# Scores in four PSUM banks, three attention groups a batch, and the context sum carried as one row by DMA

## The chip, the cores and the metric

The kernel runs on one core of one Trainium2 chip. The metric is the device time of one execution in microseconds (us). The engines named below are PE (TensorE: matrix products), DVE (VectorE), ACT (ScalarE), POOL (GpSimd) and SP (SyncE, which here only issues DMAs). ACT issues DMAs too, from a queue of its own. PSUM has eight banks of 128 partitions x 512 fp32 columns; PE writes there, and DVE and ACT read it.

## The reference, cut to what matters

There are 16 batches of 256 tokens and 512 features. Each batch goes through a gated linear attention with 8 heads, a residual and a layer norm; then it is multiplied by a decayed running sum of the squared context, with a residual and a layer norm again. A feed-forward stage with 8 experts follows; it takes over half of the time and the change does not touch it. The running sum is this part:

```
kv = jnp.swapaxes(k * v, 0, 1)          # k = v = ctx_1024: the square of the context
def step(r, kv_t):
    r = DECAY * r + kv_t                # DECAY = 0.9, over the 256 tokens of a batch
    return (r, r)
_, rs = jax.lax.scan(step, r0, kv)
return q * jnp.swapaxes(rs, 0, 1)
```

The attention is `M = M * f_t + g_t * scale * k_t v_t`, `y_t = (q_t M) * o_t`. The kernel writes it as scores k q, weighted with decays, times v.

## The kernel before

**Steps.** The attention stage is a pipeline over batches. Step b (`body(b)` on each engine) projects batch b (q, k, v, gates) and attends batch b-1, projects it out, and ends batch b-2 (layer norms, product with the sum). Steps 2 to 13 are a loop of two steps an iteration, the others are written out. Each engine runs its own list in order; semaphores join the lists.

**PE in one step.** 24 shares of projection (`project_share(b, g)`, g = 0 to 23) in the order k, k, v, q, q, v: a q or k share is six products of 256 columns, a v share three of 512. All are made of fp32 parts: high by high, high by low, low by high (`exact_product`). Between shares stand the pieces of attention: `scores(b-1, c)` for a pair of heads c = 0 to 3, into the two banks `turn`, and `weighted_values(b-1, c)` into `y_ps` and `s_ps`. Before the change PE leaves the projection for attention five times a step: scores 0; scores 1 and values 0; scores 2 and values 1; scores 3 and values 2; values 3. Then come the gate products of batch b+1, the six products of `cross_memory(b-1)` and `project_out(b-1)` (24 products of 512 columns).

**The context sum.** ACT squares the context (`square_ctx`, in place in `c_sb`) and makes its high part `ctx_hi`; POOL makes the low part `ctx_lo` (`context_low`). `cross_memory` sums over tokens by products with a triangle of ones, `sums[:, 0]`; the first 128 tokens also go into the second 128 by two products with a square of ones, `sums[:, 1]`. ACT scales the sums back into `c_sb` (`grow_memory`), and PE may overwrite the bank only after that (`mem_grown`).

**DVE** weights the scores of a head with its decays into `probs` (`weigh`), scans the decays of the next batch (`scans`), multiplies q and k by the rope tables (`rope_parts`), and makes the low parts of y (`y_low`) and of the sums' residuals. **POOL** makes the rope tables with the output gate (`o_tables`) and rotates q and k: `rotate(b, 0)` and `(b, 1)` are k, `(b, 2)` and `(b, 3)` are q.

**SP** issues its DMAs in a fixed order. In step b: `store_rms(b+1)` (256 single fp32 numbers from SBUF to DRAM, `rms_dram`), the loads of x and xT of batch b+2 and of the context of batch b, a store of batch b-2 (`x_dram`), `spread_rms(b+1)` (`rms_rows`, which waits until the stores of `store_rms` have landed), then `move(b, 0)`, `move(b, 2)`, `move(b, 1)`, `move(b, 3)` (four DMAs each, `qkT<-rot`, where `move(b, r)` waits for `rotate(b, r)`), and `following(b+1)`: `store_o`, `spread_f`, `load_g`, `spread_o` (`o_dram`, `f_all`, `g_raw`, `rot<-o_dram`).

Of the kernel before, what the change touches and what calls it, by code (L numbers as in the profile page):

```python
# [20 lines left out]
F32 = mybir.dt.float32  # L21
# [77 lines left out]
def layer_program(nc, scope, x, xT, ctx_in, norm_w, wT, wgT, bg, woutT, bout, gamma, beta, w1, b1, w2, b2,  # L99
# [91 lines left out]
    shift = sb("shift", [P, NT])  # L191

# [9 lines left out]
    s_ps = bank("s_ps")  # L202
    y_ps = bank("y_ps")
    gate_ps = bank("gate_ps")
# [27 lines left out]
    ctx_hi_done, ctx_lo_done, mem_grown = sem("ctx_hi_done"), sem("ctx_lo_done"), sem("mem_grown")  # L232
    u_done, stats2_done, x2_done, x2_stored = sem("u_done"), sem("stats2_done"), sem("x2_done"), sem("x2_stored")
# [7 lines left out]
    def score_banks(b):  # L241

        return turn

    def value_bank(b, c):

        return (y_ps, s_ps)[c % 2]
# [8 lines left out]

    def memory(b):

        return qk_ps[:, 0:D], qk_ps[:, D:2 * D]
# [109 lines left out]
    with nc.Block() as block:  # L369
# [238 lines left out]
        def _(act):  # L608
# [35 lines left out]
            def y_high(b, c):  # L644
                act.wait_ge(y_mm, b.after(KC, c + 1))
                if b.n >= 1 and c == 0:
                    act.wait_ge(out_mm, (b - 1).after(NT, NT))
                act.activation(yT_hi[:, c, :], value_bank(b, c)[:, 0:L], ACT.Copy).then_inc(y_hi_done, 1)
# [20 lines left out]
            def square_ctx(b):  # L669
# [10 lines left out]
                act.activation(ctx_hi, c_sb[b.odd][:], ACT.Copy).then_inc(ctx_hi_done, 1)  # L680

            def grow_memory(b):

                for j in range(NT):
                    act.wait_ge(mem_mm, b.after(NT, j + 1))
                    if j == 0:
                        act.wait_ge(ctx_lo_done, b.after(1, 1))
                    act.activation(c_sb[b.odd][:, j, :], memory(b)[j], ACT.Identity, bias=one[:],  # L688
                                   scale=grow[:, j:j + 1]).then_inc(mem_grown, 1)
# [9 lines left out]
            def body(b):  # L699
# [37 lines left out]
                if b.n == 1:  # L737
                    grow_memory(b - 1)
# [7 lines left out]
                if (b - 1).within(B) and b.n != 1:  # L746
                    grow_memory(b - 1)
# [76 lines left out]
        def _(pool):  # L824
# [53 lines left out]
            def context_low(b):  # L878
# [3 lines left out]
                pool.tensor_tensor(ctx_lo, c_sb[b.odd][:], ctx_hi.bitcast(F32), ALU.subtract).then_inc(ctx_lo_done, 1)  # L882
# [18 lines left out]
            def rotate(b, r):  # L901
                pool.wait_ge(rope_done, b.after(NB, r + 1))
                if b.n >= 1 and r in (0, 2):
                    pool.wait_ge(s_mm, (b - 1).after(NH, NH // 2 * (r // 2 + 1)))
# [12 lines left out]
            def body(b):  # L917
# [27 lines left out]
                if b.within(B) and b.n >= 1:  # L945
                    rotate(b, 0)
                    rotate(b, 1)
                if b.n == 1:
# [83 lines left out]
        def _(dve):  # L1032
# [49 lines left out]
            def scan(b, n):  # L1082

                dve.wait_ge(f_cleared, b.after(1, 1))
                if b.n >= 1:
                    dve.wait_ge(probs_done, (b - 1).after(NH, n + 1))
# [30 lines left out]
            def weigh(b, n):  # L1117
                dve.wait_ge(s_mm, b.after(NH, n + 1))
                dve.wait_ge(decay_done, b.after(NH, n + 1))
                if n >= 4:  # L1120
                    dve.wait_ge(y_mm, b.after(KC, (n - 4) // 2 + 1))
                elif b.n >= 1:
                    dve.wait_ge(y_mm, (b - 1).after(KC, (n + 4) // 2 + 1))
                dve.tensor_tensor(probs[:, n % 4, :], score_banks(b)[n % 2][:, 0:DW], decays[:, n, :], ALU.mult).then_inc(probs_done, 1)

            def y_low(b, c):
                dve.wait_ge(y_hi_done, b.after(KC, c + 1))
                dve.tensor_tensor(yT_lo[:, c, :], value_bank(b, c)[:, 0:L], yT_hi[:, c, :].bitcast(F32),
                                  ALU.subtract).then_inc(y_lo_done, 1)
# [31 lines left out]

            def weigh_pair(b, c):
                weigh(b, 2 * c)
                weigh(b, 2 * c + 1)
# [38 lines left out]
            def second(b):  # L1203
# [6 lines left out]
                y_low(b - 1, 0)  # L1210
# [5 lines left out]
                y_low(b - 1, 1)  # L1216
# [4 lines left out]
                y_low(b - 1, 2)  # L1221
                rope_parts(b, 2)
                y_low(b - 1, 3)
# [8 lines left out]
            def middle(b, last):  # L1232
                weigh_pair(b - 1, 0)
                add_memory(b - 2)
                norm_stats(b - 2, 1)
                weigh_pair(b - 1, 1)
                rope_parts(b, 0)
                y_low(b - 1, 0)
# [3 lines left out]
                weigh_pair(b - 1, 2)  # L1242
                token_gates(b)
                gate_v(b, 0)
                if last:
                    token_stats()
                    token_means()
                y_low(b - 1, 1)
# [3 lines left out]
                weigh_pair(b - 1, 3)  # L1252
                rope_parts(b, 2)
                y_low(b - 1, 2)
                rope_parts(b, 3)
                scans(b, 4 if last else 6)
                y_low(b - 1, 3)
# [17 lines left out]
            def behind(b):  # L1275
# [5 lines left out]
                y_low(b, 0)  # L1281
                weigh_pair(b, 2)
                add_memory(b - 1)
                y_low(b, 1)
                weigh_pair(b, 3)
                norm_stats(b - 1, 1)
                y_low(b, 2)
                split_hidden(Step(0), 0)
                y_low(b, 3)
# [107 lines left out]
        def _(pe):  # L1397
# [47 lines left out]
            def project_share(b, g):  # L1445
# [14 lines left out]
                elif part == 0 and n == 1 and b.n >= 2:  # L1460
                    pe.wait_ge(mem_grown, (b - 2).after(NT, j + 1))
# [23 lines left out]
            def scores(b, c):  # L1485
# [5 lines left out]
                if c == 0 and b.n >= 1:  # L1491
                    pe.wait_ge(probs_done, (b - 1).after(NH, NH))
                if c >= 1:
                    pe.wait_ge(probs_done, b.after(NH, 2 * c))
                halves = (slice(0, DH), slice(DH, 2 * DH))
                for rows, bank in zip(halves, score_banks(b)):
                    pe.matmul(bank[:, 0:P], kT[rows, c, P:L], qT[rows, c, P:L], start=True, stop=True)
                for rows, bank in zip(halves, score_banks(b)):
# [229 lines left out]
```

## Time and profile before

| | |
|---|---|
| time, median of 3 runs | 1248.84 us (1248.21 to 1250.78) |
| span of the profiled execution | 1250.1 us |
| PE busy | 1230.2 us (98%) |
| DVE, POOL, ACT busy | 780.7, 740.3, 460.8 us |
| steps 2 to 14 of the attention stage | from 67.92 to 496.24 us in the trace |
| two neighbouring steps of the loop begin at | 333.98 and 366.37 us |

The profiled execution's own time is its span; what lies around it is not in the trace. It stands 1.3 us (0.1%) over the median. A busy PE is a PE with a product in flight: products are pipelined, so a wait shorter than some 0.2 us does not show as idle time.

### The profile page before, as it was taken

The page shows a single profiled execution, that of the slowest core. Times are in us where ns is not written, and L with a number is a line of the kernel's source. Part 1 is how long each engine was busy: PE and PEld are TensorE (multiplying, and loading weights), DVE is VectorE, ACT ScalarE, POOL GpSimd, SP SyncE. Part 2 cuts the span into 40 slices and gives each one's busy share as a digit, 9 for nine tenths or more (in the row PEclk, how much of TensorE's full clock was granted, in tenths as well). Part 3 has the DMA queues.
Part 4 walks back from the last instruction along what each step waited for, and adds up shares of the span by engine and source line. Part 5 has one row for each costly group of instructions (what it writes and reads, how often), then busy time and mean ns, then how long its engine had stood idle before and what let it go on. Part 6 is the DMA issues. An engine that isn't in the chain of part 4 may idle for free.

```text
span 1250.1 us, 19325 instructions
## 1 busy us (share of the span) xinstructions
PE 1230.2 (98%) x6682; PEld 1011.4 (81%) x6682; DVE 780.7 (62%) x1297; ACT 460.8 (37%) x629; POOL 740.3 (59%) x519
## 2 busy tenths in 40 slices
PE   8989999999999999999999999999999999999998
PEld 7777888888888888778888888888888888888886
DVE  5887888888888888973544534543734535435424
ACT  5223333333233332353434434433534344343330
POOL 4876566666666666648538357274294385483651
PEclk9999999999999999999999999999999999999999
DMA  8778777777877776636307325235164073163310
GB/s 278 157 152 163 163 160 153 161 163 159 161 155 159 153 141 112 189 128 248 114 10 267 101 84 211 85 138 175 66 208 170 0 277 101 34 246 99 111 59 34
DMA packets 178107, 179.52 MB, mean 144 GB/s; under 512 B 44732, under 2 KB 121484, under 8 KB 178060
## 3 DMA queue, kind: packets, MB, share of 16 engines
q1 hardware_dynamic: 177548, 178.64, 53.3%
q8 instruction: 29, 0.48, 0.1%
q10 hardware_dynamic: 512, 0.26, 0.1%
q14 instruction: 18, 0.15, 0.0%
HBM read 137.55 MB, written 17.18 MB: 124 GB/s over the span
## 4 chain that ended last, share of the span: by engine, by line
PE 57%; DVE 2%; POOL 1%; issue 1%; DMA 0%; ACT 0%; POOLq 0%; DVEq 0%; ACTq 0%
PE qk_ps L89 5%; PE qk_ps L88 5%; PE qk_ps L87 5%; PE v_ps L87 5%; PE v_ps L89 5%; PE v_ps L88 5%; PE gate_ps L87 5%; PE gate_ps L89 5%; PE gate_ps L88 5%; PE s_ps L87 3%; PE s_ps L89 3%; PE s_ps L88 3%; PE y_ps L87 2%; PE y_ps L89 2%; PE y_ps L88 2%
## 5 line engine op out<-in xcount | busy, mean ns | idle before, releaser
L1006 POOL TENSOR_TENSOR w_lo<-w_raw,w_hi 128x2048 fp32r<-128x2048 f32 x31 | 143.2, 4620 | 97.8 <-ACT w_hi L760 97.8
L1342 DVE CAST hid_hi<-gate_ps 128x512 fp32r<-128x512 f32 x62 | 42.8, 690 | 193.6 <-ACT gate_ps L800 187.5
L998 POOL TENSOR_TENSOR w_lo<-w_raw,w_hi 128x2048 fp32r<-128x2048 f32 x32 | 147.7, 4617 | 12.3 <-ACT w_hi L770 12.3
L87 PE MATMUL qk_ps<-xT_parts,wqkv_hi 128*128 128x256 f32 x512 | 149.4, 292 | 2.4 <-ACT c_both L688 1.5
L1088 DVE TENSOR_TENSOR_SCAN decays<-f_all,diag 128x384 f32<-128x384 f32 x128 | 149.3, 1204 | 0.6
L88 PE MATMUL qk_ps<-xT_parts,wqkv_hi 128*128 128x256 f32 x512 | 145.4, 284 | 0.0
L89 PE MATMUL qk_ps<-xT_parts,wqkv_lo 128*128 128x256 f32 x512 | 145.2, 284 | 0.0
L1342 DVE CAST hid_hi<-v_ps 128x512 fp32r<-128x512 f32 x62 | 42.8, 690 | 141.2 <-ACT v_ps L800 141.2
L800 ACT ACTIVATE v_ps<-v_ps,b_cols 128x512 f32<-128x512 f32 x64 | 42.3, 662 | 191.0 <-PE v_ps L89 190.6
L87 PEld LDWEIGHTS qk_ps<-xT_parts,wqkv_hi 128*128 128x128 f32 x512 | 98.4, 192 | 13.3 <-issue 7.9
L800 ACT ACTIVATE gate_ps<-gate_ps,b_cols 128x512 f32<-128x512 f32 x64 | 42.2, 659 | 171.2 <-PE gate_ps L89 170.2
L970 POOL TENSOR_TENSOR rstd_b<-mean_var_b,ln_eps_b 128x4 f32<-128x4 f32 x15 | 3.0, 203 | 163.9 <-DVE mean_var_b L1318 160.9
L87 PE MATMUL v_ps<-xnT_hi,w_hi 128*128 128x512 f32 x256 | 99.8, 390 | 0.3 <-issue 0.3
L87 PE MATMUL gate_ps<-xnT_hi,w_hi 128*128 128x512 f32 x256 | 99.8, 390 | 0.0
L906 POOL TENSOR_TENSOR rot<-rot 128x256 f32<-128x256 f32 x64 | 60.1, 940 | 66.7 <-DVE rot L1115 66.4
L88 PE MATMUL gate_ps<-xnT_lo,w_hi 128*128 128x512 f32 x256 | 99.6, 389 | 0.0
L88 PE MATMUL v_ps<-xnT_lo,w_hi 128*128 128x512 f32 x256 | 99.6, 389 | 0.0
L89 PE MATMUL v_ps<-xnT_hi,w_lo 128*128 128x512 f32 x256 | 99.6, 389 | 0.0
L89 PE MATMUL gate_ps<-xnT_hi,w_lo 128*128 128x512 f32 x256 | 99.6, 389 | 0.0
L88 PEld LDWEIGHTS qk_ps<-xT_parts,wqkv_hi 128*128 128x128 f32 x512 | 98.5, 192 | 1.1
L89 PEld LDWEIGHTS qk_ps<-xT_parts,wqkv_lo 128*128 128x128 f32 x512 | 98.5, 192 | 0.0
L88 PE MATMUL qk_ps<-w_lo,hid_hi 128*128 128x512 f32 x248 | 96.5, 389 | 0.0
(238 smaller groups left out, 3220.9 us busy)
## 6 DMA issues: line engine op xcount, KB each, us to landing
w_raw<-in_w SPq DMA_DIRECT2D x64, 1024.0 KB, 7.7
f_all<-f_dram SPq DMA_DIRECT2D x16, 1024.0 KB, 4.9
qkT<-rot SPq DMA_DIRECT2D x256, 64.0 KB, 2.0
xT_raw<-in_xT SPq DMA_DIRECT2D x16, 512.0 KB, 12.7
x_both<-in_x SPq DMA_DIRECT2D x16, 512.0 KB, 11.5
f_all<-f_dram SPq DMA_DIRECT2D x16, 512.0 KB, 6.0
c_both<-in_ctx_in SPq DMA_DIRECT2D x16, 512.0 KB, 13.4
x_both<-x_dram SPq DMA_DIRECT2D x8, 1024.0 KB, 5.0
```

Source lines behind the costliest of these rows:

```text
L87: eng.matmul(out, lhs_hi, rhs_hi, start=first, stop=False)
L88: eng.matmul(out, lhs_hi, rhs_lo, start=False, stop=False)
L89: return eng.matmul(out, lhs_lo, rhs_hi, start=False, stop=last)
L800: act.activation(up_ps[c % 2][:], up_ps[c % 2][:], ACT.Gelu, bias=b1_cols[:, bass.ds(e.after(FC, c), 1)]).then_inc(gelu_done, 1)
L906: pool.tensor_tensor(a[:, 0, :], a[:, 0, :], s[:, 1, :], ALU.subtract)
L970: pool.tensor_tensor(e_rstd[n][:], e_mean_var[n][:, :, 1], e_ln_eps[:], ALU.add).then_inc(e_var_eps[n], 1)
L998: pool.tensor_tensor(w2_lo[s % 2][:], w2_raw[s % 2][:], w2_hi[s % 2][:].bitcast(F32), ALU.subtract)\
L1006: pool.tensor_tensor(w1_lo[s % 2][:], w1_raw[s % 2][:], w1_hi[s % 2][:].bitcast(F32), ALU.subtract)\
L1088: dve.tensor_tensor_scan(decays[:, n, :], f_all[:, n, :], diag[:], 0.0, ALU.mult, ALU.add).then_inc(decay_done, 1)
L1342: dve.tensor_copy(high, up_ps[c % 2][:]).then_inc(hid_hi_done, 1)
```

## The change

Four PSUM banks (`turn[0]`, `turn[1]`, `s_ps`, `gate_ps`) become one tensor `score_ps` of four banks. In steps 2 to 15 (batches 1 to 14, `in_fours`) scores 0 and 1 stand together in all four, then scores 2 and 3; attention comes in three groups, behind shares 4, 10 and 21. DVE weights a pair of heads in one instruction of 768 columns. The values of head pairs 0 and 1 share the bank `y_ps`, those of 2 and 3 the bank `s_ps`, and ACT and DVE split y in two halves of 512 columns instead of four of 256. For batches 1 to 13 (`carried`) the two products with `sums[:, 1]` are gone. The first half is summed behind share 16 (`first_memory`), ACT copies the last 32 rows of the result to SBUF and sends its last row by a DMA from its own queue to partition 0 (`carry_row`); POOL adds it to the first token of the second half (`add_carry`); ACT and POOL make the high and low part of that half (`second_high`, `second_low`), and PE sums it between the two halves of `project_out` (`second_memory`). The sums lie in `turn` instead of `qk_ps`. SP's program is unchanged.

```diff
-    turn = [bank(f"turn{n}") for n in range(2)]
+    score_ps = bank("score_ps", 2048)
+    score_banks = score_ps[:].rearrange("p (n c) -> p n c", c=D)
+    turn = [score_banks[:, n, :] for n in range(2)]
+    s_ps, gate_ps = score_banks[:, 2, :], score_banks[:, 3, :]
...
+    def in_fours(b):
+        return b.i is not None or 1 <= b.n <= B - 2
...
+    def carried(b):
+        return b.i is not None or 1 <= b.n <= B - 3
...
+            def carry_memory(b):
+                act.wait_ge(mem_mm, b.after(NT, 1))
+                act.wait_ge(sumsq_done, (b + 2).after(NT, NT))
+                act.activation(carry_rows, memory(b)[0][P - LOW_ROW:P, :], ACT.Copy).then_inc(carry_out, 1)
+                act.wait_ge(carry_out, (b - 1).after(1, 1))
+                act.dma_start(carry_row, carry[P - 1:P, :]).then_inc(carry_in, 16)
+                grow_memory(b, 0)
+            def second_high(b):
+                act.wait_ge(carry_added, (b - 1).after(1, 1))
+                act.activation(ctx_hi[:, 1, :], c_sb[b.odd][:, 1, :], ACT.Copy).then_inc(second_hi_done, 1)
...
                 for c in range(KC):
-                    if (b - 1).within(B):
-                        y_high(b - 1, c)
+                    if (b - 1).within(B) and c % 2:
+                        y_high(b - 1, c // 2)
+                    if (b - 1).within(B) and carried(b - 1):
+                        if c == 1:
+                            carry_memory(b - 1)
+                        elif c == 2:
+                            second_high(b - 1)
...
+            def add_carry(b):
+                pool.wait_ge(carry_in, (b - 1).after(16, 16))
+                pool.wait_ge(ctx_squared, b.after(NT, NT))
+                first = c_sb[b.odd][0:1, 1, :]
+                pool.tensor_tensor(first, first, carry_row, ALU.add).then_inc(carry_added, 1)
+            def second_low(b):
+                pool.wait_ge(second_hi_done, (b - 1).after(1, 1))
+                pool.tensor_tensor(ctx_lo[:, 1, :], c_sb[b.odd][:, 1, :], ctx_hi[:, 1, :].bitcast(F32),
+                                   ALU.subtract).then_inc(second_lo_done, 1)
...
                     rotate(b, 0)
                     rotate(b, 1)
+                if (b - 1).within(B) and carried(b - 1):
+                    add_carry(b - 1)
+                    second_low(b - 1)
...
             def middle(b, last):
-                weigh_pair(b - 1, 0)
                 add_memory(b - 2)
                 norm_stats(b - 2, 1)
+                weigh_pair(b - 1, 0)
                 weigh_pair(b - 1, 1)
...
+            def attend(b, g):
+                if g == 4:
+                    scores(b, 0)
+                    scores(b, 1)
+                elif g == 16 and carried(b):
+                    first_memory(b)
+                elif g == 10:
+                    weighted_values(b, 0)
+                    weighted_values(b, 1)
+                    scores(b, 2)
+                    scores(b, 3)
+                elif g == 21:
+                    weighted_values(b, 2)
+                    weighted_values(b, 3)
...
                 for j in range(NT):
+                    if j == 1 and carried(b):
+                        second_memory(b)
...
+            def first_memory(b):
+                pe.wait_ge(ctx_lo_done, b.after(1, 1))
+                pe.wait_ge(probs_done, b.after(KC, 3))
+                now = memory(b)[0]
+                pe.matmul(now, sums[:, 0, :], ctx_hi[:, 0, :], start=True, stop=False)
+                pe.matmul(now, sums[:, 0, :], ctx_lo[:, 0, :], start=False, stop=True).then_inc(mem_mm, 1)
```

POOL, in a step of the loop, before: the low part of the whole context (L882), the output-gate tables (L898, L899), then the four rotations (the first of them stands here; two instructions each, `rot` is q and k with the tables), then the output gate's rows (`REGISTER_ALU` and `ISA` rows, of registers alone, are left out).

```order
L882 TENSOR_TENSOR ctx_parts<-c_both,ctx_parts 128x1024
...
L898 TENSOR_TENSOR rot<-rot,rope_sb 128x512
L899 TENSOR_TENSOR rot<-rot,rope_sb 128x512
...
L906 TENSOR_TENSOR rot<-rot 128x256
L907 TENSOR_TENSOR rot<-rot 128x256
...
L892 TENSOR_TENSOR o_rows<-gates,rms_rows 24x256
```

The same place now, up to the rotation that `move(b, 2)` waits for (L962 and L963 are the rotations, L933 is `add_carry`, L937 is `second_low`):

```order
L924 TENSOR_TENSOR ctx_parts<-c_both,ctx_parts 128x512
...
L955 TENSOR_TENSOR rot<-rot,rope_sb 128x512
...
L962 TENSOR_TENSOR rot<-rot 128x256
L963 TENSOR_TENSOR rot<-rot 128x256
...
L933 TENSOR_TENSOR c_both<-c_both,squares 1x512
L937 TENSOR_TENSOR ctx_parts<-c_both,ctx_parts 128x512
...
L962 TENSOR_TENSOR rot<-rot 128x256
L963 TENSOR_TENSOR rot<-rot 128x256
```

Half of the low part has moved behind the second rotation, and in front of it stands an addition that waits for a DMA; the third and fourth rotation, those of q, stand behind both.

ACT, in a step of the loop, before, from the first y part (L648) to the scaling of the sums (L688):

```order
L648 ACTIVATE yT_hi<-y_ps 128x256
...
L648 ACTIVATE yT_hi<-s_ps 128x256
L648 ACTIVATE yT_hi<-y_ps 128x256
L648 ACTIVATE yT_hi<-s_ps 128x256
L654 ACTIVATE gates_sum<-gate_ps 24x256
L665 ACTIVATE gates<-gates_sum,gate_bias 24x256
L667 DMA f_dram<-gates 16x256
L688 ACTIVATE c_both<-qk_ps,one,memory_raw 128x512 x2
```

The same place now (L704 copies the rows, L706 sends the row in 16 pieces of 32 numbers, L712 is `second_high`, L662 a half of y):

```order
L662 ACTIVATE yT_hi<-y_ps 128x512
L704 ACTIVATE squares<-score_ps 32x512
L706 DMA squares<-squares 1x16x32
L722 ACTIVATE c_both<-score_ps,one,memory_raw 128x512
L712 ACTIVATE ctx_parts<-c_both 128x512
L662 ACTIVATE yT_hi<-score_ps 128x512
L669 ACTIVATE gates_sum<-score_ps 24x256
L680 ACTIVATE gates<-gates_sum,gate_bias 24x256
L682 DMA f_dram<-gates 16x256
L722 ACTIVATE c_both<-score_ps,one,memory_raw 128x512
```

The second half of y and all that follows on ACT now stand behind L712, which waits for the row.

## Rows read from the trace of the kernel before

**Rows 1.** The page: head, and busy time with its share of the span.
```profile
span 1250.1 us, 19325 instructions
PE 1230.2 (98%) x6682; PEld 1011.4 (81%) x6682; DVE 780.7 (62%) x1297; ACT 460.8 (37%) x629; POOL 740.3 (59%) x519
```

**Rows 2.** PE's waits: us in total, times, longest us.
```profile
PE turn L1497 <- DMA qkT<-rot: 4.2, 2, 3.1
...
PE qk_ps L87 <- ACT c_both L688: 1.5, 1, 1.5
```

**Rows 3.** PE timeline into and out of attention: start, us, instruction, count.
```profile
275.81 0.28 PE L88 MATMUL qk_ps<-xT_parts,wqkv_hi 128*128 128x256 f32 x1
275.93 0.28 PE L89 MATMUL qk_ps<-xT_parts,wqkv_lo 128*128 128x256 f32 x1
276.14 0.49 PE L1497 MATMUL turn<-qkT 64*128 64x128 f32 x4
...
277.80 0.50 PE L87 MATMUL v_ps<-wqkv_hi,xT_parts 128*128 128x512 f32 x1
278.13 0.40 PE L88 MATMUL v_ps<-wqkv_lo,xT_parts 128*128 128x512 f32 x1
278.37 0.40 PE L89 MATMUL v_ps<-wqkv_hi,xT_parts 128*128 128x512 f32 x1
```

**Rows 4.** PE timeline: the first products of steps 2, 10, 11 and 15.
```profile
67.92 0.39 PE L87 MATMUL qk_ps<-xT_parts,wqkv_hi 128*128 128x256 f32 x1
...
333.98 0.28 PE L87 MATMUL qk_ps<-xT_parts,wqkv_hi 128*128 128x256 f32 x1
...
366.37 0.28 PE L87 MATMUL qk_ps<-xT_parts,wqkv_hi 128*128 128x256 f32 x1
...
496.24 0.28 PE L87 MATMUL qk_ps<-xT_parts,wqkv_hi 128*128 128x256 f32 x1
```

**Rows 5.** SP timeline: its DMA issues in a step that begins at 333.98.
```profile
334.46 0.48 SPq L422 DMA_DIRECT2D o_dram<-o_rows  x1
...
343.07 0.83 SPq L396 DMA_DIRECT2D rms_dram<-rms  x2
...
359.48 7.50 SPq L440 DMA_DIRECT2D qkT<-rot  x12
367.02 0.48 SPq L422 DMA_DIRECT2D o_dram<-o_rows  x1
```

**Rows 6.** DMA view of 345 to 360 us: GB/s in 40 slices of 0.375 us.
```profile
GB/s 49 126 251 11 0 0 0 5 49 60 60 60 44 27 11 16 27 22 27 33 11 27 33 27 164 279 339 227 235 232 366 396 396 421 404 393 391 369 229 183
```

**Rows 7.** The tile view of qkT, 52 to 60 us: four small DMAs, issue to landing.
```profile
DMA to landing us min/median/max: 10.7/11.1/11.4
```

**Rows 8.** DMA queues (packets, MB): 55:64 (first row), 64:66 (the others).
```profile
q1 hardware_dynamic: 124, 0.25, 97.4%
...
q8 instruction: 1, 0.02, 3.1%
q14 instruction: 2, 0.02, 2.4%
```

**Rows 9.** DMA view of 86 to 101 us: GB/s in 40 slices of 0.375 us.
```profile
GB/s 1 2 0 71 202 164 0 0 0 0 0 44 44 55 66 55 44 11 27 33 22 5 33 44 16 22 137 213 347 265 227 227 306 390 396 415 421 382 377 402
```

**Rows 10.** The page, DMA issues: KB each, median us to landing.
```profile
f_dram<-gates ACTq DMA_DIRECT2D x16, 16.0 KB, 1.6
```

**Rows 11.** POOL timeline: a table of 512 columns, and a rotation of q.
```profile
27.43 1.30 POOL L898 TENSOR_TENSOR rot<-rot,rope_sb 128x512 f32<-128x512 f32 x1 [1.11 <-DMA rot<-o_dram]
...
358.01 0.74 POOL L906 TENSOR_TENSOR rot<-rot 128x256 f32<-128x256 f32 x1 [4.78 <-DVE rot L1115]
358.70 0.75 POOL L907 TENSOR_TENSOR rot<-rot 128x256 f32<-128x256 f32 x1
```

**Rows 12.** ACT timeline: two copies of 512 columns from PSUM, one of 1024 from SBUF.
```profile
331.91 1.45 ACT L688 ACTIVATE c_both<-qk_ps,one,memory_raw 128x512 f32<-128x512 f32 x2 [0.55 <-ACT gates L665]
...
336.93 1.06 ACT L680 ACTIVATE ctx_parts<-c_both 128x1024 fp32r<-128x1024 f32 x1
```

More of the change, by code:

```diff
@@ L255, in sum_of @@
         return xb[1] if b.i is None and b.n == B - 1 else res
+    def carried(b):
+        return b.i is not None or 1 <= b.n <= B - 3
     def memory(b):
-        return qk_ps[:, 0:D], qk_ps[:, D:2 * D]
+        return turn if carried(b) else (qk_ps[:, 0:D], qk_ps[:, D:2 * D])
     def steps(eng, body):
@@ L679, in square_ctx, with grow_memory @@
                     act.wait_ge(wout_lo_done, 1)
-                act.activation(ctx_hi, c_sb[b.odd][:], ACT.Copy).then_inc(ctx_hi_done, 1)
-            def grow_memory(b):
-                for j in range(NT):
+                if carried(b):
+                    act.activation(ctx_hi[:, 0, :], c_sb[b.odd][:, 0, :], ACT.Copy).then_inc(ctx_hi_done, 1)
+                else:
+                    act.activation(ctx_hi, c_sb[b.odd][:], ACT.Copy).then_inc(ctx_hi_done, 1)
+            def carry_memory(b):
[8 more added lines that the diff above has]
+                act.activation(ctx_hi[:, 1, :], c_sb[b.odd][:, 1, :], ACT.Copy).then_inc(second_hi_done, 1)
+            def grow_memory(b, *halves):
+                for j in halves:
                     act.wait_ge(mem_mm, b.after(NT, j + 1))
@@ L947, in body @@
                     rotate(b, 1)
+                if (b - 1).within(B) and carried(b - 1):
+                    add_carry(b - 1)
+                    second_low(b - 1)
                 if b.n == 1:
@@ L1460, in project_share @@
                 elif part == 0 and n == 1 and b.n >= 2:
+                    pe.wait_ge(rope_done, (b - 1).after(NB, j + 3))
                     pe.wait_ge(mem_grown, (b - 2).after(NT, j + 1))
@@ L1557, in project_out, with second_memory @@
                     mm.then_inc(out_mm, 1)
+            def first_memory(b):
[4 more added lines that the diff above has]
+                pe.matmul(now, sums[:, 0, :], ctx_lo[:, 0, :], start=False, stop=True).then_inc(mem_mm, 1)
+            def second_memory(b):
+                pe.wait_ge(second_lo_done, (b - 1).after(1, 1))
+                pe.wait_ge(probs_done, b.after(KC, 3))
+                later = memory(b)[1]
+                pe.matmul(later, sums[:, 0, :], ctx_hi[:, 1, :], start=True, stop=False)
+                pe.matmul(later, sums[:, 0, :], ctx_lo[:, 1, :], start=False, stop=True).then_inc(mem_mm, 1)
             def cross_memory(b):
@@ L1576, in body @@
             def body(b):
-                for n in range(NH):
-                    slot(b, n)
+                if b.within(B) and in_fours(b - 1):
+                    for g in range(3 * NH):
+                        project_share(b, g)
+                        attend(b - 1, g)
+                else:
+                    for n in range(NH):
+                        slot(b, n)
                 if b.n == B:
@@ L1582, in body @@
                     gate_products(b + 1)
-                if (b - 1).within(B) and 2 <= b.n <= B - 2:
-                    cross_memory(b - 1)
                 if (b - 1).within(B):
```

130 lines of the change are left out of this document (71 added, 59 removed).

## Prediction

> **What bounds the kernel now.** I read the page's busy times first: PE is busy for 98% of the span, DVE, POOL and ACT for 62, 59 and 37% [rows 1]. So the second view is the one of PE's waits. In the attention stage it shows 4.2 us for `qkT` (3.1 of it once, in step 2) and 1.5 us for the bank of the context sum (once, in step 3) [rows 2], and nothing that returns in each step. The timeline of PE then gives the pace: one loop step is 366.37 - 333.98 = 32.4 us, and PE's list fills it [rows 4]. Within it, products of 256 columns follow each other every 0.12 us and those of 512 every 0.23 to 0.24 us [rows 3]. What PE no longer has to do is therefore gained, as long as no other list needs more than the shorter step. That second question decides here, and SP's timeline and the DMA view answer it.
>
> **What PE saves.** Two products of 512 columns less in steps 2 to 14: 2 x 0.23 = 0.46 us a step. A change between projection and attention costs about 0.09 us going in (0.21 us from product to product where 0.12 is usual) and 0.09 to 0.10 us coming out (0.33 us where 0.24 is usual) [rows 3]; three groups instead of five save 2 x 0.19 = 0.38 us, in steps 2 to 15. So a step of PE alone is 32.4 - 0.84 = 31.5 us. Over 13 steps that is 10.9 us. In step 2 the first scores now stand three shares (18 products, 2.2 us) later, so that the wait of 3.1 us for `qkT` shrinks to about 0.9; the wait of 1.5 us in step 3 goes, because the sum no longer lies in `qk_ps` [rows 2]. Step 15 gives about 1 us: 0.4 of changes, and the rest because weights and halves of y cost DVE fewer instructions there. Sum: 10.9 + 2.2 + 1.5 + 1 = 15.6 us. That is the whole gain if nothing else is late: 1250.1 - 15.6 = 1234.5 in the trace.
>
> **Covers that hold.** The longer groups need DVE earlier: scores 0 and 1 end 5.4 us into the step, DVE has both pairs weighted by about 7.4 (it first ends batch b-2), and values 0 come at 9.7. Scores 2 and 3 end at 13.2, their values stand behind share 21, at 21.5. This costs nothing; without that cover it would be about 1 us a step. The last half of y is copied and split by ACT and DVE, 0.7 us each [rows 12], after values 3 at 23.2; `project_out` wants it with its third share of j = 0, at 27.0. POOL has 1.5 us more to do (three instructions of 512 columns, about 1.3 us each [rows 11], for one of 1024) and is idle for 40% of the time [rows 1]: nothing by itself. What counts is what waits where.
>
> **The row by DMA, and what stands behind it.** `first_memory` stands behind share 16, 17.6 us into the step (17 shares of 0.7 us, and two groups of 1.9 and 3.5). With the two products and ACT's copy of 32 rows the DMA leaves at about 19. Until it lands, ACT is held at `second_high` and behind it the second half of y; POOL is held at `add_carry`, and behind that stand both rotations of q. Behind these stand SP's `move(b, 2)`, `move(b, 1)`, `move(b, 3)`, and behind those everything that SP issues next. PE itself waits if the row lands later than 23.5: from then 1.3 (`add_carry`) + 0.55 (`second_high`, half of 1.06) + 0.7 + 0.7 (y) + 0.2 for the handing over = 3.5 us bring us to the 27.0 at which y is due.
>
> When does it land? A DMA of ACT's own queue takes 1.6 us in this trace [rows 10], but those of the loop leave behind the gates, late in a step. This one leaves elsewhere. SP issues the 256 single numbers of `store_rms` at 343.07 and the loads right behind them [rows 5]. From 346.1 to 354.0 the DMA engines then deliver nearly nothing (0 to 60 GB/s, against 160 to 420 behind it), and at 354.0 all goes on at once [rows 6]. In step time this jam lasts from 12 to 20, and step 2 has it too, until 95.8 [rows 9]. The row leaves at 19, inside it. Four small SBUF to SBUF DMAs of SP that left in the jam of step 1 took 11 us to land [rows 7]. That is SP's queue. Whether another queue is held too, no row shows directly; the nearest is that the instruction fetches, which have queues of their own, are absent from the 9 us of that jam, and three come within 2 us behind it [rows 8]. I take it that the row is held until the jam ends.
>
> The Trainium skill ("DMA: Bandwidth & Descriptors", section on queues, rings and completion order) says that the queues of SP and ACT use the same sixteen engines, that an engine takes turns between queues by whole packets, and that the write of a semaphore lands only after every earlier write of that engine, across its queues. By that rule the row, which goes out in sixteen pieces, waits for the slowest engine and the time is that of the forecast below; by the 1.6 us of [rows 10] alone it would be 1233.
>
> A row that is held closes a loop. From its landing to the start of `move(b, 2)`: 1.3 + 0.55 + 1.3 (`second_low`) + 1.44 (the rotation, 358.01 to 359.45) + 0.2 = 4.8 us [rows 11, 12]. The twelve moves: 7.5 us. From there to the end of the next jam: 354.0 - 334.46 = 19.5 us, SP's own list until 343.07 and then the jam [rows 5, 6]. Then the row lands r later. The loop is 4.8 + 7.5 + 19.5 + r = 31.8 + r us a step, whatever PE does, against 31.5 that PE needs and 32.4 before. Before, the rotation of q hung on DVE alone and this loop was open.
>
> No row shows r. From below: when the jam ends only the tail of the flight is left, some 0.4 us. From above: a whole flight of 1.6 - 0.3 = 1.3 us behind the issue [rows 10], and 0.5 for POOL when it meets DVE's scans (one rotation of q there took double the time of the other), so 1.8. I take 1.2, between the middle and the upper end, because sixteen pieces must land behind the loads that all start at the same moment [rows 6]. The loop is then 33.0 us.
>
> **The sum.** The first row lands at 95.8 + 1.2 = 97.0 (step 2, where PE then waits some 5 us). The thirteenth, in step 14, 12 x 33.0 = 396 us later, at 493.0. From a landing to the end of the step: 3.5 to the split y, then 6 products of j = 0, `second_memory` and 12 products of j = 1, 20 x 0.23 = 4.6: 8.1 us. Step 15 begins at 501.1 instead of 496.24: 4.9 us later. Less 1 us in step 15: 3.9 us, 1254.0 in the trace. The profiled execution stands 1.3 us over the median; in the measure of the runs I say 1252.7, slower by 0.3%.
>
> **The rivals.**
> *The row is not held.* ACT's queue gets its turn in the jam and the row lands by 22, before PE needs it. For it: the 1.6 us, and that no row shows a DMA of ACT in the jam. Against it: the missing instruction fetches. Then the loop is open, SP's list (about 30 us of work a step) has room, and the time is 1234.5 - 1.3 = 1233. This ends on the other side; the point from which it decides is a landing before 23.5 in step time.
> *The row is held, but lands at once when the jam ends.* With r = 0.5 the loop is 32.3: first row 96.3, the last at 483.9, step 15 at 492.0, 4.2 us earlier than before, and with step 15's 1 us 1244.9 in the trace, 1243.6 as a median. At r = 0.9 it is even. At r = 1.8 the loop is 33.6 and the same sum gives 1262 in the trace.
>
> **How the numbers follow.** Held with r of 0.9 to 1.8, my forecast: 0.5. Not held: 0.25. Held with r under 0.9: 0.25, of which half lie within 0.2%. About 0.2% (2.5 us) is what a measurement of this kernel tells from no change. Of the forecast's 0.5, 0.43 lie over it and 0.07 within; so slower 0.43, same 0.2, faster 0.37. The range goes from the case of the open loop, 1231, to r = 1.8 in each step, 1262; the forecast's own range is 1249 (r = 0.9) to 1261 (r = 1.8).
>
> **What would show it.** Right: in the loop, landing times of the row (issue at 19, landing at 24 to 26 in step time); POOL idle before L933 until the DMA; ACT's second y half late, PE waiting in `project_out` for y or in front of `second_memory` by 1 to 1.5 us in each step; steps of about 33 us. The six products of the sum become four, and attention stands in three groups, in either case. Wrong: the row landing about 2 us after its issue with the jam still on, steps of 31.5 us and no wait of PE in the loop; then the reading of the jam as one that stops every queue has failed. If the jam itself is gone or lies elsewhere, the 19.5 us have failed.

## The result, and the profile after

The changed kernel takes 1307.07 us (median of 4 runs, 1306.18 to 1310.49) where the kernel before took 1249.81 beside it: a ratio of 1.0471, 95% interval 1.045 to 1.0491. It is slower, to which the prediction gave a chance of 0.43, but by 57 us and not by 4.

The page after: head, and busy time [rows 1].

```profile
span 1304.4 us, 19086 instructions
PE 1231.2 (94%) x6656; PEld 1017.9 (78%) x6656; DVE 780.7 (60%) x1201; ACT 465.5 (36%) x623; POOL 759.3 (58%) x545
```

The view of waits after (us in total, times, longest us), where [rows 2] had two single waits of PE:

```profile
ACT ctx_parts L712 <- POOL c_both L933: 114.1, 13, 10.8
...
POOL c_both L933 <- DMA squares<-squares: 89.8, 13, 8.3
...
PE y_ps L87 <- DVE yT_lo L1190: 55.8, 15, 6.1
```

The chain can be read backwards: PE waits 15 times for the low part of y, DVE for ACT's high part, ACT (`second_high`, L712) for POOL's `add_carry` (L933), POOL for the row. A step of the loop shows it in time. The timeline after (start, us, instruction, idle before and releaser), of POOL, ACT, DVE, PE and SP in the step that begins at 361.61, with the landings of the row in other steps:

```profile
99.27 1.25 POOL L933 TENSOR_TENSOR c_both<-c_both,squares 1x512 f32<-1x512 f32 x1 [7.57 <-DMA squares<-squares]
...
361.61 0.28 PE L87 MATMUL qk_ps<-xT_parts,wqkv_hi 128*128 128x256 f32 x1
...
375.02 0.82 SPq L410 DMA_DIRECT2D rms_dram<-rms  x2
...
377.30 0.37 SPq L473 DMA_DIRECT2D c_both<-in_ctx_in  x1
...
379.93 0.52 ACTq L706 DMA_DIRECT2D squares<-squares  x1
390.67 1.25 POOL L933 TENSOR_TENSOR c_both<-c_both,squares 1x512 f32<-1x512 f32 x1 [7.78 <-DMA squares<-squares]
391.95 0.63 ACT L712 ACTIVATE ctx_parts<-c_both 128x512 fp32r<-128x512 f32 x1 [10.60 <-POOL c_both L933]
392.49 0.58 ACT L662 ACTIVATE yT_hi<-score_ps 128x512 fp32r<-128x512 f32 x1
...
393.10 0.69 DVE L1190 TENSOR_TENSOR yT_lo<-score_ps,yT_hi 128x512 fp32r<-128x512 f32 x1 [5.31 <-ACT yT_hi L662]
393.84 0.80 PE L87 MATMUL y_ps<-wout_hi,yT_hi 128*128 128x512 f32 x1 [5.78 <-DVE yT_lo L1190]
393.88 0.73 POOL L962 TENSOR_TENSOR rot<-rot 128x256 f32<-128x256 f32 x1
...
403.06 0.48 SPq L436 DMA_DIRECT2D o_dram<-o_rows  x1
...
426.92 1.27 POOL L933 TENSOR_TENSOR c_both<-c_both,squares 1x512 f32<-1x512 f32 x1 [7.29 <-DMA squares<-squares]
...
533.40 1.25 POOL L933 TENSOR_TENSOR c_both<-c_both,squares 1x512 f32<-1x512 f32 x1 [2.86 <-DMA squares<-squares]
542.74 0.28 PE L87 MATMUL qk_ps<-xT_parts,wqkv_hi 128*128 128x256 f32 x1
```

The row leaves 18.3 us into the step (379.93) and POOL has it at 390.67. The rotation of q (L962) stands behind it, and SP has issued all its moves at 403.06. This is the loop of the prediction; its pace is (533.40 - 99.27) / 12 = 36.2 us a step, where 33.0 was said.

The DMA view after, of 371 to 395 us (GB/s in slices of 0.6 us, then issues with KB each and us to landing; [rows 6] of before):

```profile
GB/s 360 347 333 35 16 164 133 128 1 1 154 119 0 0 17 82 61 38 3 38 44 14 20 41 188 328 227 273 383 405 406 387 333 200 184 31 0 0 0 0
...
x_both<-in_x SPq DMA_DIRECT2D x1, 512.0 KB, 11.0
...
c_both<-in_ctx_in SPq DMA_DIRECT2D x1, 512.0 KB, 13.5
...
squares<-squares ACTq DMA_DIRECT2D x1, 2.0 KB, 10.7
```

The jam is there and ends at 385.4 (the slice of 188 GB/s, as 354.0 was that of 164 before). But the row, 2 KB, lands at 379.93 + 10.7 = 390.6, and the context, which SP issued at 377.30, at 377.30 + 13.5 = 390.8: the row comes in with the loads that were issued ahead of it, 5.2 us behind the jam's end. This step, of 39.7 us, is one of the long ones (the others of the loop take 33.9 to 39.8); the tile view gives the row's time in all thirteen:

```profile
DMA to landing us min/median/max: 7.2/8.1/11.0
```

However long it takes, it lands within 0.5 us of that step's context in twelve of the thirteen steps; in the last, where no x is loaded, it lands 1.5 us behind the context and 0.2 us behind the store of x2. Why the row comes with these is the question for the experiments.

From step 15 on the kernel loses as well: 753.9 us before (1250.1 - 496.24), 761.7 after (1304.4 - 542.74). The timeline of PE after, behind step 15's start:

```profile
571.03 0.79 PE L87 MATMUL y_ps<-wout_hi,yT_hi 128*128 128x512 f32 x1 [3.24 <-DVE yT_lo L1190]
...
583.59 0.49 PE L1558 MATMUL score_ps<-qkT 64*128 64x128 f32 x4 [3.74 <-ACT c_both L722]
```

The 3.74 us are the scores' new wait for `mem_grown`, here for batch 14, whose sum doesn't lie in their banks; the other is y in halves, which makes PE wait once more, for 1.27 us at 602.40. With the groups alone (the first experiment below) the same two waits for y are 1.76 and 1.25 us; the rest of the 3.24 has no run of its own.

### The profile page after: what moved, and what is told of

Its sections match the earlier page's. It is cut to its first block, busy times and chain, and to the rows that moved or that the text cites. A ratio compares the mean times of both kernels' runs of the same rounds, so it can differ in the third digit from the quotient of the medians.

```text
span 1304.4 us, 19086 instructions
## 1 busy us (share of the span) xinstructions
PE 1231.2 (94%) x6656; PEld 1017.9 (78%) x6656; DVE 780.7 (60%) x1201; ACT 465.5 (36%) x623; POOL 759.3 (58%) x545
## 4 chain that ended last, share of the span: by engine, by line
PE 78%; DMA 11%; DVE 3%; ACT 2%; POOL 2%; issue 2%; SPq 2%; POOLq 0%; ACTq 0%; DVEq 0%
DMA squares<-squares 9%; PE qk_ps L87 8%; PE score_ps L87 8%; PE score_ps L88 8%; PE score_ps L89 8%; PE qk_ps L89 8%; PE qk_ps L88 8%; PE v_ps L87 6%; PE v_ps L88 5%; PE v_ps L89 5%; PE y_ps L87 3%; PE y_ps L89 3%; PE y_ps L88 3%; PE score_ps L1560 2%; PE score_ps L1558 1%
## 5 line engine op out<-in xcount | busy, mean ns | idle before, releaser
L1394 DVE CAST hid_hi<-score_ps 128x512 fp32r<-128x512 f32 x62 | 42.8, 690 | 193.8 <-ACT score_ps L841 187.8
L87 PE MATMUL qk_ps<-xT_parts,wqkv_hi 128*128 128x256 f32 x512 | 147.1, 287 | 1.1 <-DVE wqkv_lo L1102 0.9
L88 PE MATMUL qk_ps<-xT_parts,wqkv_hi 128*128 128x256 f32 x512 | 144.5, 282 | 0.0
L1147 DVE TENSOR_TENSOR_SCAN decays<-f_all,diag 128x384 f32<-128x384 f32 x128 | 136.8, 1106 | 0.7
L841 ACT ACTIVATE score_ps<-score_ps,b_cols 128x512 f32<-128x512 f32 x64 | 42.2, 659 | 171.1 <-PE score_ps L89 170.1
L87 PE MATMUL score_ps<-xnT_hi,w_hi 128*128 128x512 f32 x256 | 99.8, 390 | 0.0
L89 PE MATMUL score_ps<-xnT_hi,w_lo 128*128 128x512 f32 x256 | 99.6, 389 | 0.0
L88 PE MATMUL score_ps<-xnT_lo,w_hi 128*128 128x512 f32 x256 | 99.6, 389 | 0.0
L87 PE MATMUL qk_ps<-w_hi,hid_hi 128*128 128x512 f32 x248 | 96.5, 389 | 0.0
```

The costliest lines, as they stand in the source:

```text
L87: eng.matmul(out, lhs_hi, rhs_hi, start=first, stop=False)
L88: eng.matmul(out, lhs_hi, rhs_lo, start=False, stop=False)
L89: return eng.matmul(out, lhs_lo, rhs_hi, start=False, stop=last)
L841: act.activation(up_ps[c % 2][:], up_ps[c % 2][:], ACT.Gelu, bias=b1_cols[:, bass.ds(e.after(FC, c), 1)]).then_inc(gelu_done, 1)
L1147: dve.tensor_tensor_scan(decays[:, n, :], f_all[:, n, :], diag[:], 0.0, ALU.mult, ALU.add).then_inc(decay_done, 1)
L1394: dve.tensor_copy(high, up_ps[c % 2][:]).then_inc(hid_hi_done, 1)
```

## The experiments

**The groups alone.**

```diff
     def carried(b):
-        return b.i is not None or 1 <= b.n <= B - 3
+        return False
...
                     pe.wait_ge(probs_done, (b - 1).after(KC, KC))
-                    pe.wait_ge(mem_grown, (b - 1).after(NT, NT))
...
                     gate_products(b + 1)
+                if (b - 1).within(B) and 2 <= b.n <= B - 2:
+                    cross_memory(b - 1)
```

> Four banks and three groups stay; the sum is again made by six products in front of project_out, into qk_ps, and no row is sent. Theory (the row's loop is what costs): no loop is left, a step costs PE 32.4 - 3 x ... that is 32.36 - 0.38 = 32.0 us, so step 15 begins some 5 to 7 us earlier than before (2 of it from step 2's first scores); from step 15 on it stays some 4 us longer than before, because y in halves waits there for ACT and DVE: about 1247 us, ratio 0.997. Rival (the longer groups or DVE's wide weights cost it, not the row): steps stay near 36 us, 1300 or more.

1238.9 us, ratio 0.9918 (0.9905 to 0.9932). The row and the waits that come with it are what costs (this kernel also leaves out the scores' wait for `mem_grown`, priced below), and the groups gain more than expected (1247 us): the view of windows shows one step with its length, busy times, granted clock, DMA share and GB/s.

```profile
325.93:357.28 31.35, 31.35 (x224) 26.60 (x222) 28.33 (x43) 9.68 (x17) 21.29 (x22) 1.00 0.79 161
```

31.35 against 32.4 us: 1.0 us, where the working had 0.38. PE's timeline says why; first before, then with the groups alone.

```profile
340.86 0.49 PE L1497 MATMUL turn<-qkT 64*128 64x128 f32 x4
...
341.71 0.65 PE L1512 MATMUL y_ps<-probs,v 128*64 128x256 f32 x4
...
342.51 0.50 PE L87 MATMUL v_ps<-wqkv_hi,xT_parts 128*128 128x512 f32 x1
```

```profile
335.54 0.65 PE L1571 MATMUL y_ps<-probs,v 128*64 128x256 f32 x4
...
337.00 0.49 PE L1557 MATMUL score_ps<-qkT 64*128 64x128 f32 x4
...
338.51 0.50 PE L87 MATMUL v_ps<-wqkv_hi,xT_parts 128*128 128x512 f32 x1
```

Eight products of scores took 0.85 us to the next kind of product and eight of values 0.80; sixteen in one go take 1.51 and 1.46. Twice 0.19 and twice 0.14 are 0.66 us, and with the 0.38 of the changes from and to the projection 1.04.

**The loop opened.**

POOL's list, then ACT's, then PE's:

```diff
-                if (b - 1).within(B) and carried(b - 1):
-                    add_carry(b - 1)
-                    second_low(b - 1)
...
                     rotate(b, 3)
+                if (b - 1).within(B) and carried(b - 1):
+                    add_carry(b - 1)
+                    second_low(b - 1)
...
-                        elif c == 2:
-                            second_high(b - 1)
...
                     gate_low(b + 1)
+                if (b - 1).within(B) and carried(b - 1):
+                    second_high(b - 1)
...
-                    pe.wait_ge(mem_grown, (b - 1).after(NT, NT))
+                    if carried(b - 1):
+                        pe.wait_ge(mem_grown, (b - 1).after(NT, NT))
...
-                    if j == 1 and carried(b):
-                        second_memory(b)
...
                     mm.then_inc(out_mm, 1)
+                if carried(b):
+                    second_memory(b)
```

> The row stays, but those that wait for it no longer stand in front of the rotations of q and of y: POOL's add_carry and second_low behind rotate(b, 2) and (b, 3), ACT's second_high behind y's second half and gate_low, PE's second_memory behind all of project_out; and the scores wait for mem_grown only where the sum lies in their banks. Theory: the row lands as late as before against its issue (5 to 7 us), but no list that sets the pace waits: steps of 31.5 to 31.9 us, step 15 begins at 484 to 490 us instead of 542.7; after it some 4 us more than before: 1240 to 1248 us, ratio about 0.995. Rival (the six to four products are not what the row holds; SP's list or second_memory is next): steps of 32.4 us or more, ratio 1.00 or above.

1229.85 us, ratio 0.9851 (0.9836 to 0.9866): the fastest kernel of this study, 1.5% under the kernel before and below the 1240 to 1248 expected. Windows, one step of the loop:

```profile
288.19:319.04 30.85, 30.85 (x222) 26.19 (x221) 27.61 (x44) 10.53 (x18) 23.09 (x24) 1.00 0.81 164
```

PE is busy for the whole step of 30.85 us, 0.5 less than with the groups alone: the two products. The row still lands 5.8 us after its issue, at 24 in step time; nothing that sets the pace stands behind it. From step 15 on it takes 754.6 us (1227.9 - 473.27), where 4 us more than before had been expected and 0.7 came.

**No single-number stores.**

```diff
-    sp.dma_start(rms_dram[b.odd, j * P:(j + 1) * P].rearrange("(p a) -> p a", a=1), rms[:, b.odd, j:j + 1])
+    sp.dma_start(rms_dram[b.odd, j * P:(j + 1) * P].rearrange("(a p) -> a p", a=1), rope_sb[0:1, 0, 0:P])
```

> As the changed kernel, but store_rms writes 128 neighbouring numbers of one partition (two transfers of 512 bytes each, of a table) instead of 256 single numbers; so the gates and all that hangs on them are wrong, and only the time is looked at. Theory (the single numbers cause the jam and the row waits for what stands ahead of it): no stretch of under 60 GB/s behind L396, the loads are down when the row leaves, the row lands 2 to 3 us after its issue, steps of 31.5 to 32 us, about 1247 us. Rival (a row of ACT's queue in this place takes 7 to 11 us whatever SP stores): the loop stays, 35 us or more a step, 1295 or more.

1251.11 us, ratio 1.0028 (1.0015 to 1.0041). The DMA view of 334 to 352 us (the row leaves at 343.66):

```profile
x_both<-in_x SPq DMA_DIRECT2D x1, 512.0 KB, 3.4
...
x_dram<-res SPq DMA_DIRECT2D x1, 512.0 KB, 7.5
...
squares<-squares ACTq DMA_DIRECT2D x1, 2.0 KB, 5.4
```

Without the single numbers the loads land after 3.4 to 7.5 us and not 11 to 14.3: they make the jam. But the expected 2 to 3 us for the row did not come. The loads and the store, issued 14 to 16 us into the step, were still under way, and it landed at 349.1, 0.3 us behind the last of them, the store of x2 (341.26 + 7.5 = 348.8); in twelve of the thirteen steps it is 0.2 to 0.9 us. In the thirteenth, where the loads were down before it left, it took 1.6 us. So loads hold the row without any single numbers too. The steps became 30.85 to 35.6 us.

**The loads later.**

```diff
                 if (b + 1).within(B):
                     store_rms(b + 1)
+                if (b + 1).within(B) and b.n < B - 1:
+                    spread_rms(b + 1)
+                    move(b, 0)
                 if (b + 2).within(B):
                     load_x(b + 2)
                     load_xT(b + 2)
...
-                if (b + 1).within(B):
-                    spread_rms(b + 1)
```

> As the changed kernel, but SP issues x, xT, the context and the store of x2 behind spread_rms and move(b, 0), not behind store_rms: when the row leaves, only the single-number stores stand in the queues ahead of it. Theory (the 4.5 us between the jam's end and the landing are the loads that SP issued before the row): the row lands 0.5 to 1.5 us after the jam's end, the loop is 32.3 to 33.3 us, the time 1255 to 1268 (some us more if the later loads are missed by ACT). Rival (4.5 us is the row's own flight behind a jam): the loop stays at 36 us, 1300 to 1307.

1245.94 us, ratio 0.9992 (0.9974 to 1.0009): 61 us less than the changed kernel, and more than expected, since the loop falls under PE's own step (30.85 to 31.9 us). What is still lost against the opened loop lies mostly behind step 15: 763.8 us there (1243.5 - 479.71) and not 754.6. The timeline of SP, ACT and POOL in the step that begins at 323.09:

```profile
335.00 0.82 SPq L410 DMA_DIRECT2D rms_dram<-rms  x2
341.41 0.52 ACTq L708 DMA_DIRECT2D squares<-squares  x1
342.78 0.33 SPq L416 DMA_DIRECT2D rms_rows<-rms_dram  x1
343.12 1.69 POOL L935 TENSOR_TENSOR c_both<-c_both,squares 1x512 f32<-1x512 f32 x1 [0.19 <-DMA squares<-squares]
```

The row is there 1.7 us after its issue, and no load of x or of the context had been issued ahead of it. The single numbers landed at nearly the same time (`spread_rms`, L416, waits for them), so whether they would have held it for longer stays open here.

**A probe, sent too early.** With the groups alone, and SP's order once as in the experiment before and once as it was:

```diff
     scale_x2(b - 2)
+    act.dma_start(carry_row, rope_sb[P - 1:P].rearrange("p s t -> p (s t)")).then_inc(carry_in, 16)
```

> Groups alone, SP's loads behind move(b, 0), and a probe: in steps 2 to 14 ACT sends one row of 2 KB (of the rope table, to the partition that the changed kernel's row goes to; nobody needs it) right behind scale_x2, some 11 us into the step, when the 256 single numbers have just been issued and no load stands ahead. Theory (a row waits for the loads issued ahead of it, and the single numbers alone don't hold it): it lands about 1.7 us later, at 13. Rival (the single numbers hold ACT's queue too): it lands when they have landed, 7 us after its issue, at 17 to 19.

> Groups alone with SP's order as it was, and the same probe at the same place: behind the single numbers, between the issues of the loads. Theory: the loads issued ahead of it hold it until they land, 10 to 13 us, at 21 to 24 in step time, though it is 2 KB. Rival (turns between the queues): 1.7 us, or at the latest with the end of the jam, 17 to 18.

The second misses its purpose: ACT reaches this place at 9.7 and not at 11, within 0.5 us of the single numbers and ahead of the loads (1236.1 and 1235.77 us, one run each). Of the single numbers both tell something. The packets of the row go out 1.2 us behind its issue in either case, but it has landed only when all its sixteen pieces have counted on the semaphore. Issued 0.25 us or more ahead of the single numbers, it lands after 1.7 to 2.2 us (five cases); issued 0.15 us or more behind them, after 6.8 to 8.4 us, within 1 us of their landing (nine cases whose counts the trace has complete). That is the rival of the first expectation.

**The probe in the middle of the jam.**

```diff
+    act.wait_ge(v_mm, b.after(NT, 1))
     act.dma_start(carry_row, rope_sb[P - 1:P].rearrange("p s t -> p (s t)")).then_inc(carry_in, 16)
```

> The probe with SP's loads behind move(b, 0), but sent behind the first half of v, 13.5 us into the step: the single numbers were issued 4 us earlier and are not landed before 17 to 18, and no load has been issued. Theory (single numbers that are not yet landed do not hold a row between SBUF partitions, only loads ahead of it in the engines do): its packets go out 1.2 to 1.4 us behind the issue, at 15. Rival (the jam of the single numbers holds every queue, as the prediction took it): 17 to 19.

> The same probe at 13.5 us with SP's order as it was: x, xT and the context were issued 10.4 to 12 us into the step and cannot land before 21 to 25. Theory: the probe's packets stand behind theirs on each engine and go out at 21 to 24, 8 to 10 us behind the issue, though the row of the changed kernel, sent 5 us later, goes out at the same time. Rival (a flight of its own, or turns by packet between the queues): 15, or 17 to 19 where the jam alone holds it.

With the single numbers alone, SP's and ACT's timeline, and the DMA view of 340.8 to 341.2 us (queue, packets, MB, share; q10 is ACT's):

```profile
335.49 0.82 SPq L410 DMA_DIRECT2D rms_dram<-rms  x2
339.71 0.52 ACTq L765 DMA_DIRECT2D squares<-rope_sb  x1
343.35 0.33 SPq L416 DMA_DIRECT2D rms_rows<-rms_dram  x1
```

```profile
q10 hardware_dynamic: 32, 0.00, 5.0%
```

All 32 packets of the row go out between 1.1 and 1.5 us behind its issue, 2 us before the single numbers have landed. That is what the theory said of the packets. The landing, which is what POOL waits for in the changed kernel, did not come with them: of the row's sixteen counts in the trace the first stands at 341.21 and the last at 343.51, 17.4 us into the step, 0.18 us behind the last count of the single numbers (343.33). In all ten steps whose counts are complete it is 0.17 to 0.20 us. So the rival holds for the landing: single numbers ahead of the row hold it until they have landed, here 3.2 to 5.7 us behind its issue.

With the loads ahead, ACT's and SP's timeline and the DMA view of 336 to 354 us:

```profile
336.40 0.37 SPq L473 DMA_DIRECT2D c_both<-in_ctx_in  x1
338.00 0.52 ACTq L763 DMA_DIRECT2D squares<-rope_sb  x1
```

```profile
c_both<-in_ctx_in SPq DMA_DIRECT2D x1, 512.0 KB, 13.7
...
squares<-rope_sb ACTq DMA_DIRECT2D x1, 2.0 KB, 12.0
```

The same row lands after 12.0 us, at 350.0, and the context at 336.40 + 13.7 = 350.1. Between 338.0 and 345.9 the queue view shows no packet of q10 at all, and the first goes out at 347.35. So leaving nearly five us earlier in the step than the changed kernel's row brought it in no earlier: it lands 15.9 us behind the issue of the single numbers (334.13), the row of the changed kernel 15.6 us (375.02). It comes with the loads, 6.5 us behind the single numbers. The two runs, one execution each, are two arms of one question: this arm is as its theory said, the other one by its packets alone.

**POOL's part of the opening alone.**

```diff
-                if (b - 1).within(B) and carried(b - 1):
-                    add_carry(b - 1)
-                    second_low(b - 1)
...
                     rotate(b, 3)
+                if (b - 1).within(B) and carried(b - 1):
+                    add_carry(b - 1)
+                    second_low(b - 1)
```

> As the changed kernel, but POOL's add_carry and second_low stand behind rotate(b, 2) and (b, 3); ACT and PE are left as changed. Theory (the loop runs through the rotations of q and SP's moves): the loop is open; the row lands at 24, POOL adds it behind the rotations at 25.1 to 26.4, second_high 27, y's second half by ACT 27.7 and DVE 28.4, so PE waits 1 to 1.5 us a step before the third share of project_out: steps of 32 to 33 us, and a time of 1250 to 1265. Rival (y's second half behind second_high is what costs, the rotations nothing): steps stay at 35 us or more, 1295 or more.

1280.84 us, ratio 1.0253 (1.0236 to 1.027): neither the 1250 to 1265 of the theory nor the 1295 of its rival. The loop is open (steps of some 33.5 and 35.0 us, nearly in turn, 36.2 with the loop), but PE's wait for the second half of y is 2.3 us in every step, not 1 to 1.5: POOL ends the rotations at 25.6, half a us later than worked out, and PE comes to its third share at 26.5, half a us sooner. And in five of the twelve steps from 3 on the clock falls behind that wait. Windows: two steps, then what follows the wait of 2.30 us that ends at 340.3.

```profile
311.59:346.64 35.05, 32.75 (x221) 27.28 (x220) 27.50 (x43) 11.58 (x22) 22.63 (x24) 0.95 0.73 151
346.64:380.14 33.50, 31.14 (x221) 26.15 (x220) 27.12 (x43) 9.18 (x16) 22.61 (x24) 1.00 0.72 143
```

```profile
340.30:344.00 3.70, 3.64 (x9) 2.88 (x10) 2.89 (x6) 0.51 (x2) 0.68 (x2) 0.54 0.39 99
```

A wait of 2.3 us thus costs 2.6 us (33.50 - 30.85) in a step where the clock stays and 4.2 where it falls.

**The tail's wait.**

```diff
-    pe.wait_ge(mem_grown, (b - 1).after(NT, NT))
+    if carried(b - 1):
+        pe.wait_ge(mem_grown, (b - 1).after(NT, NT))
```

> As the changed kernel, but the scores wait for mem_grown only where the sum of the batch before lies in their banks, that is not for batch 14, whose sum lies in qk_ps. Theory: PE's wait of 3.7 us in front of the scores of batch 15 goes and what follows comes that much earlier: about 1303 us, ratio to before 1.044. Rival (ACT and DVE are late there anyway and the wait moves to the values or to y): 1307.

1301.29 us, ratio 1.0419 (1.0401 to 1.0436). The wait of 3.74 us is gone; from step 15 on it takes 759.2 us (1297.1 - 537.93) and not 761.7, because the wait for y in step 15 is 4.79 us here, not 3.24. So 2.5 of the 3.7 us are kept. The rest of the 6 us lies in the loop, whose steps scatter from 34.4 to 37.6 us behind the first of them; this edit does not explain that part.

## Why the prediction was right in kind and wrong in size

**The step that failed is r, the landing of the row behind the jam's end.** The prediction had the loop as 4.8 + 7.5 + 19.5 + r. Measured in one turn: from the landing (390.6) to SP's second move (395.5) 4.9, the twelve moves to 403.0 7.5, from there to the next jam's end (421.6) 18.6. These three hold within 1 us. But r was taken as 1.2 with bounds of 0.4, which no row gave, and 1.8, "the tail of the flight" and "a whole flight", and is 4.4 to 5.3 (3.0 in the last step): 36.2 and not 33.0 us a step. Over twelve steps that is 38 of the 50 us by which the trace missed. The prediction saw that the sixteen pieces "must land behind the loads", but it priced this by the flight of another row and not by the landing of the 1.5 MB of loads that SP had issued into the jam. The probe in the middle of the jam shows that these loads make the difference between a row that lands with the single numbers and one that lands 6.5 us behind them.

The trace of before had the number. Its DMA view of 342 to 362 us gives the landing of the loads:

```profile
x_both<-in_x SPq DMA_DIRECT2D x1, 512.0 KB, 11.6
...
c_both<-in_ctx_in SPq DMA_DIRECT2D x1, 512.0 KB, 13.9
```

SP issued the context there at 345.36, so that it landed at 359.3, 5.3 us behind the jam's end at 354.0. "What else is in flight when this transfer leaves, and when does that land" would have made r 5.3, the loop 37.1 and, by the prediction's own sum, the time about 1306 us. That this comes so near to 1307 is partly luck: the loop takes 36.2, and the tail below, missed too, makes up for it.

**Why the row was held.** "I take it that the row is held until the jam ends" names one holder of two. Single numbers that have not landed do hold the row: with no load ahead its last count came 0.18 us behind theirs. Loads hold it as well: without single numbers it landed 0.2 to 0.9 us behind the store of x2. In the changed kernel both stand ahead, and the loads decide, because they land later (the single numbers by 383.1, the context at 390.8). The missing instruction fetches [rows 8] were a sign of this, or of chance: no run here says which. The rule of the Trainium skill that the prediction weighed ("DMA: Bandwidth & Descriptors", "Queues, rings and completion order") has an engine take turns between the queues it has work for by whole packets, and a semaphore's write land only after every earlier write of that engine, across its queues. With the second half the probe behind the single numbers agrees (packets out 2 us before, last count 0.18 us behind). From the first half the probe behind the loads differs: none of its packets went out for 7.9 us, in which 322 of SP's queue did. Why not, no run here tells.

**The first landing** was put at 97.0 and is 99.2: r is 5.2 there too, and the jam of step 2 ends at 94.0, 1.8 us earlier than said, which hides part of it. **The end of the step** behind the last landing took 9.4 us (533.3 to 542.74), not 8.1.

**The tail.** "Step 15 gains 1 us" failed too: it and what follows lose 7.8 us. Two costs were missing in the list of waits that the change adds, the scores' wait for `mem_grown` where it isn't needed (the run without it keeps 2.5 us) and the later second half of y. The trace misses by 2.2 + 38.1 + 1.3 + 8.8 = 50.4 us in all, from 1254.0 to 1304.4.

**PE's saving** was set at 0.84 us a step and is 1.5: 0.5 for the two products (0.46 said), 1.0 for the groups (0.38 said), because a change of kind inside a group costs as well. It was of no use in the changed kernel, where the loop sets the pace.

**What held.** The place of PE's wait (`project_out`, the third share), the order of those held (POOL, ACT's second half of y, the rotations of q, SP's moves), the covers for DVE's wide weights, step 2's smaller wait (1.4 us for `qkT`) and the missing wait of step 3. The rival with an open loop was 1233 us; opened, the kernel takes 1229.85, though not because its row lands early: it lands at 24, late by that rival's own mark of 23.5. What stands behind the row decided, not the row.

## What to carry to other kernels

In these kernels a row of 2 KB landed when what had been issued ahead of it landed, single numbers or loads, also from another queue: its price is read from the landing times of the transfers in flight at its place, not from its own flight elsewhere. That its packets are out is not that it has landed. Before a wait for it is put into an engine's list, see what that list still has to do for the transfers themselves; here what waits for the row moved behind the rotations, y and `project_out`, together with the tail's wait dropped, turned 4.7% slower into 1.5% faster. And a wait that PE meets in each step is to be priced with the clock behind it.

## What the runs showed of the hardware

Single numbers hold loads, but not by keeping the engines busy. The DMA view of the kernel with later loads, 330 to 352 us (GB/s in slices of 0.55 us):

```profile
GB/s 387 384 347 349 335 37 7 117 143 145 70 1 0 0 0 0 0 0 0 0 0 0 2 2 0 0 30 52 190 194 82 209 410 378 367 322 140 58 35 67
```

The single numbers, issued at 335.00, landed just before 342.78, and for 5.5 us of this nothing moves. The packets of a row between SBUF partitions that is sent then go out at once, as the probe showed, but its last count comes 0.2 us behind theirs. Loads issued into this time land 11 to 14 us after their issue. Why a read from DRAM is held by them, no run here tells.

PE's clock was the other surprise. Windows of the changed kernel from the wait of 5.78 us on, which ends at 393.84 (the column behind POOL's is the granted clock):

```profile
394.00:396.00 2.00, 2.00 (x5) 1.61 (x6) 1.87 (x4) 0.00 (x0) 2.00 (x3) 0.50 0.00 0
...
398.00:400.00 2.00, 2.00 (x7) 1.58 (x6) 0.00 (x0) 2.00 (x4) 0.26 (x1) 0.55 0.43 115
400.00:402.00 2.00, 2.00 (x14) 1.76 (x13) 0.46 (x1) 1.95 (x4) 0.00 (x0) 1.00 0.42 107
```

For some 6 us behind the wait PE runs at the lower level, 1.2 GHz, though it is busy again. In the changed kernel this should cost nothing more, since the loop sets the pace and the slower products only eat into the next wait; that is argued, and no run tests it. With POOL's part alone it costs some 1.5 us (35.05 against 33.50) in five of twelve steps, behind a wait of 2.3 us; in the others a wait of the same length left the clock at 1.00.
